# Second cross-attention of a perceiver stack: three PSUM places for scores, a split last chunk and another order around the maximum

## The reference, cut to what matters

```python
scale = 1.0 / np.sqrt(ATT_DIM).astype(np.float32)
Q = jnp.einsum('bld,de->ble', input_1, Wq) + bq
K = jnp.einsum('bld,de->ble', input_2, Wk) + bk
V = jnp.einsum('bld,de->ble', input_2, Wv) + bv
scores = jnp.einsum('bqd,bkd->bqk', Q, K) * scale
scores = jnp.clip(scores, -100.0, 100.0)
weights = jax.nn.softmax(scores, axis=-1)
return jnp.einsum('bqk,bkd->bqd', weights, V)
```

## Time and profile before

| | us |
|---|---|
| median of 3 runs | 1199.65 |
| lowest and highest | 1196.90, 1203.51 |
| the profiled execution, device time | 1200.66 |
| its span in the profile | 1198.9 |
| TensorE / VectorE / ScalarE / GpSimd busy, share of the span | 95% / 76% / 75% / 49% |
| mean granted TensorE clock | 0.993 |

### The profile page before, as it was taken

The page is one execution under the profiler, slowest core; times in us unless marked ns, Lnnn a source line. Parts: engine busy times, 40 slices in busy tenths (PEclk is TensorE's granted clock), DMA queues, the critical chain, the costliest instruction groups (busy, mean ns, idle before and its releaser), DMA issues. The chain is left out here.

```text
span 1198.9 us, 32157 instructions
## 1 busy us (share of the span) xinstructions
PE 1144.7 (95%) x12519; PEld 795.4 (66%) x12519; DVE 909.6 (76%) x1739; ACT 902.8 (75%) x1557; POOL 586.9 (49%) x548
## 2 busy tenths in 40 slices
PE   4899999999999999999999999999988999889898
PEld 2466666666666666666666666666666648744698
DVE  7677878888888888888878787877774689689632
ACT  4599988888988889888888888888881459495010
POOL 6165656665666665656556666656561250133000
PEclk8999999999999999999999999999999899999999
DMA  6365544545353535353535353534335884050284
GB/s 217 84 180 165 157 122 99 146 95 152 92 152 90 154 95 155 92 149 91 155 94 154 92 151 90 154 94 124 91 98 175 309 311 146 10 177 1 95 288 173
DMA packets 141428, 163.93 MB, mean 137 GB/s; under 512 B 18352, under 2 KB 127184, under 8 KB 141280
## 3 DMA queue, kind: packets, MB, share of 16 engines
q1 hardware_dynamic: 140736, 159.82, 46.4%
q10 hardware_dynamic: 544, 2.10, 0.5%
HBM read 72.25 MB, written 12.99 MB: 71 GB/s over the span
## 5 line engine op out<-in xcount | busy, mean ns | idle before, releaser
L468 POOL TENSOR_TENSOR pT_lo<-p_exp,pT_hi 128x896 f16<-128x896 f32 x223 | 421.3, 1889 | 319.4 <-ACT pT_hi L568 319.4
L549 ACT ACTIVATE p_exp<-ps,ln_k,esc 128x896 f32<-128x896 f32 x224 | 246.3, 1100 | 54.0 <-PE ps L910 46.1
L682 DVE TENSOR_REDUCE tile_max<-ps 128x128 f16<-128x896 f32 x224 | 244.4, 1091 | 49.5 <-PE ps L886 47.1
L568 ACT ACTIVATE pT_hi<-p_exp 128x896 f16<-128x896 f32 x224 | 211.9, 946 | 1.0
L677 DVE TENSOR_TENSOR v_lo<-ps,v_hi 128x512 f16<-128x512 f32 x196 | 135.5, 691 | 72.9 <-ACT v_hi L541 70.6
L928 PE MATMUL ps<-v_lo,pT_hi 128*128 128x64 f16 x1568 | 164.4, 193 | 0.0
L927 PE MATMUL ps<-v_hi,pT_hi 128*128 128x65 f16 x1568 | 164.3, 193 | 0.1
L873 PE MATMUL ps<-c_hi,wk_hi 128*128 128x448 f16 x448 | 159.1, 355 | 5.4 <-DVE c_lo L664 4.7
L929 PE MATMUL ps<-v_hi,pT_lo 128*128 128x65 f16 x1568 | 163.8, 193 | 0.0
L873 PE MATMUL ps<-c_lo,wk_hi 128*128 128x448 f16 x448 | 158.4, 354 | 0.0
L873 PE MATMUL ps<-c_hi,wk_lo 128*128 128x448 f16 x448 | 158.4, 354 | 0.0
(11 more groups left out here) (401 smaller groups left out, 2080.9 us busy)
## 6 DMA issues: line engine op xcount, KB each, us to landing
k_st<-k_top SPq DMA_DIRECT2D x444, 112.0 KB, 2.3
k_st<-k_rest SPq DMA_DIRECT2D x444, 56.0 KB, 2.0
c_raw<-in_ctxT SPq DMA_DIRECT2D x14, 896.0 KB, 5.9
xa_cn<-in_ctx SPq DMA_DIRECT2D x14, 896.0 KB, 6.6
me_w<-in_me_w SPq DMA_DIRECT2D x8, 1536.0 KB, 6.3
ctx_parts<-c_hi SPq DMA_DIRECT2D x14, 448.0 KB, 2.8
ctx_parts<-c_lo SPq DMA_DIRECT2D x14, 448.0 KB, 3.0
me_w<-in_me_w SPq DMA_DIRECT2D x8, 768.0 KB, 5.8
```

The source lines that it names most:

```text
L468: nc.gpsimd.tensor_tensor(pT_lo[:, n % 2, :, :].rearrange("p t s -> p (t s)"), p_exp[:, n % 2, :], pT_hi[:, n % 2, :, :].rearrange("p t s ...
L549: nc.scalar.activation(p_exp[:, n % 2, :], s_scores[n % 2], ACT.Exp, bias=ln_k[:, 0:1], scale=esc[:, n // H0 % 2:n // H0 % 2 + 1]).then_in ...
L568: nc.scalar.activation(pT_hi[:, n % 2, :, :].rearrange("p t s -> p (t s)"), p_exp[:, n % 2, :], ACT.Copy).then_inc(pT_hi_ready, 1)
L682: nc.vector.tensor_reduce(tile_max[:, n % 2, :], s_scores[n % 2].rearrange("p (t s) -> p s t", s=S), AX.X, ALU.max).then_inc(tile_max_done, 1)
```

## The change

PSUM has a third place for scores, banks 0 and 1, and TensorE waits for the chunk three back. The last two chunks are clipped after the maximum, not the last alone. The last chunk's matmuls are done one bank after the other, each counted in `scores_done`, and its maximum is taken by halves into `ends`; the maximum of the first 13 chunks is formed before. The turned tiles go to banks 0 to 3 in place of 2 to 5. VectorE makes the low parts of the first four tiles before those of the last three, and TensorE begins to weigh with the four tiles while the three are waited for at the fifth.

```diff
-        total = t("total", [P, NCH])
+        total, ends = t("total", [P, NCH]), t("ends", [P, 2])
...
-        sc_ps = [ps[:, 2:4, 0:HCH], ps[:, 4:6, 0:HCH]]
-        t_ps = [[ps[:, 2, :], ps[:, 3, :]], [ps[:, 4, :], ps[:, 5, :]]]
+        sc_ps = [ps[:, b:b + 2, 0:HCH] for b in (2, 4, 0)]
+        t_ps = [[ps[:, 0, :], ps[:, 1, :]], [ps[:, 2, :], ps[:, 3, :]]]
+        CLIPS_FIRST = NCH - 2
+        measured_all = 2 * CLIPS_FIRST + 1
...
                 def exponent(c):
...
-                    if c == NCH - 1:
-                        act.wait_ge(E["clipped"], 2 * NCH)
+                    if c >= CLIPS_FIRST:
+                        act.wait_ge(E["clipped"], measured_all + c - CLIPS_FIRST + 1)
...
                 def measure(c):
...
-                    nc.vector.tensor_reduce(chunk_max[:, c:c + 1], sc_ps[c % 2], AX.XY, ALU.max).then_inc(E["clipped"], 1)
+                    nc.vector.tensor_reduce(chunk_max[:, c:c + 1], sc_ps[c % 3], AX.XY, ALU.max).then_inc(E["clipped"], 1)
...
                 def clip(c):
...
-                    nc.vector.tensor_scalar(sc[:, c * CH:(c + 1) * CH].rearrange("p (b k) -> p b k", b=2), sc_ps[c % 2],
+                    nc.vector.tensor_scalar(sc[:, c * CH:(c + 1) * CH].rearrange("p (b k) -> p b k", b=2), sc_ps[c % 3],
...
-                for c in range(NCH - 1):
+                for c in range(CLIPS_FIRST):
...
-                measure(NCH - 1)
-                v.wait_ge(E["clipped"], 2 * NCH - 1)
+                measure(NCH - 2)
+                v.wait_ge(E["clipped"], measured_all)
+                link(nc.vector.tensor_tensor(chunk_max[:, 0:NCH - 1], chunk_max[:, 0:NCH - 1], f[:, 0:NCH - 1], ALU.mult))
+                link(nc.vector.tensor_reduce(top[:, :], chunk_max[:, 0:NCH - 1], AX.X, ALU.max))
+                link(nc.vector.tensor_scalar(top[:, :], top[:, :], lim[:, 0:1], None, ALU.max))
+                for b in range(2):
+                    v.wait_ge(E["scores_done"], NCH + b)
+                    link(nc.vector.tensor_reduce(ends[:, b:b + 1], sc_ps[(NCH - 1) % 3][:, b, :], AX.X, ALU.max))
                 marks["top"] = link.count + 1
-                link(nc.vector.tensor_tensor(chunk_max[:, :], chunk_max[:, :], f[:, :], ALU.mult))
-                link(nc.vector.tensor_reduce(top[:, :], chunk_max[:, :], AX.X, ALU.max))
-                link(nc.vector.tensor_scalar(top[:, :], top[:, :], lim[:, 0:1], lim[:, 1:2], ALU.max, ALU.min))
+                link(nc.vector.tensor_scalar(ends[:, 0:1], ends[:, 0:1], ends[:, 1:2], f[:, NCH - 1:NCH], ALU.max, ALU.mult))
+                link(nc.vector.tensor_scalar(top[:, :], ends[:, 0:1], top[:, 0:1], lim[:, 1:2], ALU.max, ALU.min))
                 nc.vector.tensor_scalar(neg_top[:, :], top[:, :], -1.0, LN_K, ALU.mult, ALU.add).then_inc(E["top_ready"], 1)
+                clip(NCH - 2)
                 clip(NCH - 1)
...
                     link(nc.vector.tensor_copy(pT_hi[:, c % 2, T0:TILES, :], turned[1]))
-                    nc.vector.tensor_tensor(pT_lo[:, c % 2, T0:TILES, :], turned[1], pT_hi[:, c % 2, T0:TILES, :], ALU.subtract).then_inc(E["pT_ready"], 1)
                     v.wait_ge(E["pT_hi_ready"], c + 1)
                     nc.vector.tensor_tensor(pT_lo[:, c % 2, 0:T0, :], turned[0], pT_hi[:, c % 2, 0:T0, :], ALU.subtract).then_inc(E["pT_ready"], 1)
+                    nc.vector.tensor_tensor(pT_lo[:, c % 2, T0:TILES, :], turned[1], pT_hi[:, c % 2, T0:TILES, :], ALU.subtract).then_inc(E["pT_ready"], 1)
...
-                    at_least(pe, E["clipped"], 2 * (c - 1))
-                    for k in range(DC):
-                        if c == 0:
-                            pe.wait_ge(E["q2_ready"], k + 1)
-                        for q2, low in ((q2_hi, 0), (q2_hi, 1), (q2_lo, 0)):
-                            for b in range(2):
-                                mm = nc.tensor.matmul(sc_ps[c % 2][:, b, :], q2[:, k, :], ct[:, low, k, b * HCH:(b + 1) * HCH],
-                                                      start=(k == 0 and low == 0 and q2 is q2_hi), stop=(k == DC - 1 and q2 is q2_lo))
-                    mm.then_inc(E["scores_done"], 1)
-                pe.wait_ge(E["clipped"], 2 * NCH - 2)
-                spin(nc, spare, ident, 4)
-                keep_warm(nc, pe, spare, ident, vlink.sem, marks["top"], marks["top"] + 2)
+                    at_least(pe, E["clipped"], 2 * (c - 2))
+                    for bs in ((0, 1),) if c < NCH - 1 else ((0,), (1,)):
+                        for k in range(DC):
+                            if c == 0:
+                                pe.wait_ge(E["q2_ready"], k + 1)
+                            for q2, low in ((q2_hi, 0), (q2_hi, 1), (q2_lo, 0)):
+                                for b in bs:
+                                    mm = nc.tensor.matmul(sc_ps[c % 3][:, b, :], q2[:, k, :], ct[:, low, k, b * HCH:(b + 1) * HCH],
+                                                          start=(k == 0 and low == 0 and q2 is q2_hi), stop=(k == DC - 1 and q2 is q2_lo))
+                        mm.then_inc(E["scores_done"], 1)
+                pe.wait_ge(E["clipped"], measured_all)
+                spin(nc, spare, ident, 3)
+                keep_warm(nc, pe, spare, ident, vlink.sem, marks["top"], marks["top"] + 1, 2)
...
                 def turn_p(c):
...
-                        pe.wait_ge(E["clipped"], 2 * NCH)
+                        pe.wait_ge(E["clipped"], measured_all + 1)
...
                 def weigh(c):
...
-                    pe.wait_ge(E["pT_ready"], 2 * c + 2)
+                    pe.wait_ge(E["pT_ready"], 2 * c + 1)
                     for tile in range(TILES):
+                        if tile == T0:
+                            pe.wait_ge(E["pT_ready"], 2 * c + 2)
...
```

## The result

| | before | after |
|---|---|---|
| median of 20 runs, us | 1199.15 | 1196.94 |
| lowest and highest | 1196.14, 1203.57 | 1194.37, 1200.41 |
| the profiled execution, device time | 1200.66 | 1194.58 |
| its span | 1198.9 | 1192.9 |

The ratio of the changed kernel to the kernel before is 0.9972, 95% interval 0.9961 to 0.9983: 3.4 us less, between 2.0 and 4.7. The two medians in the table are 2.2 us apart. The forecast was 3.1. Times of this size tell that the change gains something; how much it gains is read inside the block.

The account below looks back on a forecast made before the run. Waits between VectorE and TensorE over two PSUM places bound the scores pass, VectorE the weighing; 2.14 + 0.47 + 0.48 = 3.1 us off 1199.65 gives a median of 1196.6, range 1193.3 to 1200.2.

Parts of the forecast that it names:

- Third place: Scores pass: TensorE no longer waits for a clip to free its PSUM place; last scores end 1.70 us earlier.
- Around the maximum: From chunk 12's measure to neg_top: half maxima at 0.62 each; neg_top starts 2.14 us earlier, 2.0 to 2.3 with bounds.
- Two clips behind: After neg_top: the second clip fills VectorE's 1.22 us idle before the first cast; costs nothing, at worst 0.1.
- Order of the split: Weighing pass: low part of four tiles comes first; first weighing 0.47 us earlier, 0.48 more at the end.
- Sum: Whole block: 2.14 + 0.47 + 0.48 = 3.1 us less; the median becomes 1196.6 us.
- no difference: Whole kernel: the measurement cannot tell the change from none, bound about 0.5%; chance 0.87.
- What follows: Behind the block: ended by a barrier, its loads hang on its own steps, so it moves as a whole.
- A: Scores pass: the third place frees nothing, as loads or issue hold TensorE; gain 1.5 us, 1198.1; chance 0.10.
- B: Weighing pass: TensorE's wait at the fifth tile costs 3.9 us over 13 chunks; gain 0.4, 1199.2; chance 0.10.
- C: Scores pass or stretch before the first weighing: TensorE's clock falls; up to 31.8 us, 1228.3; chance 0.03.
- the loads: Scores pass: chunk 13's column load lands with 2.3 us of slack before TensorE wants it; costed at nothing.

Follow-up runs that it names:

- the kernel before with warming matmuls: Six identity matmuls added to TensorE's idle time in the feed-forward block ahead, on the kernel before; median 1200.13 us, ratio to before 0.9984.
- late columns: Changed kernel with the column loads of chunks 11 to 13 issued two chunks later each; 1198.21 us in one run, block 80.50 us.

## Why the prediction was right

**Third place.** Predicted 1.70 earlier, with TensorE as the bound; measured 31.17 to 29.47, and 1.69 of the block when done alone. The releaser that I took from the clip's end plus 0.11, against the view's "issue", was right: with two places the pauses came back.

**Around the maximum.** Predicted neg_top 2.14 earlier, measured 2.09. The halves were taken at 0.62 each from the 384 and 512 rows; the two take 1.28 with the gap between them, which is the same. The clamp with one limit took 0.24 with its gap, not 0.20, and the two operations before it 0.45, not 0.44. That is the missing 0.05.

**Two clips behind.** Predicted at nothing; measured nothing, by the cast at 2.49 behind neg_top with one clip and with two. It fits by 0.1 us.

**Order of the split.** Predicted 0.47 at the front and 0.48 at the end, nothing between. Measured 0.44 at the first weighing; from there to the last addition 46.01 became 45.56, 0.45, and to the last weighing 40.70 became 40.25, where 40.2 was forecast. Alone 0.86, within the change 0.89.

**Sum.** 3.09 predicted, 2.98 in the block, 3.4 (2.0 to 4.7) by the ratio. The sums of parts agree: 1.69 + 0.86 for place and order alone leave 0.43 for the early maximum, the halves and the clip together, which measured 0.40. That leaves 0.03 for the turned tiles' other banks, which have no run of their own. The forecast median, 1196.6, came within 0.4 of the 1196.94 measured; that is luck in part, since it was built on a median of three runs and the 20 runs lie 7.4 us apart for the kernel before and 6.0 for the changed one. The 3.09 against 2.98 in the block is the test of the mechanism. By the 0.5% that the prediction took as its bound, 0.28% is no difference, the case to which it gave 0.87.

**What follows** moved as a whole: 162.64 after, 162.56 before.

**Rivals.** A fell (two places make the pauses return). What A would have left, a gain of 1.5, measured 1.26 with two places, as neg_top then came 0.38 earlier and not 0.56. B fell: the fifth tile starts without a gap in every chunk, and the order alone shortens the block. C fell: the clock is 1.00 from the first measure to the last scores, with TensorE busy 29.50 of 29.50 us, and from there to the first weighing. The Trainium skill's rule on going round PSUM banks (TensorE: Matmul & The Clock Gate, "A second HAM failure mode: psum-queue depth-cycling") does not show in the traces of this case: the clock stayed at 1.00 with two places and 13 pauses, and with three places the pauses are gone.

**What was mis-sized** is a term costed at nothing. I gave the loads 2.3 us of slack on the row of 8.0 us from issue to landing. In the changed kernel the load took 10.3, and the slack was 0.9. It hid the loads all the same. By these numbers a scores pass another microsecond faster would meet them, which is an estimate.

## What to carry to other kernels

Where two engines hand a pair of buffers back and forth and the pass is slower than either engine's own need, look at the buffers: here a third place gained the number of chunks times the difference to the slower engine, 13 x (2.40 - 2.27) = 1.70 us, and this could be read off one timeline. Splitting an instruction so that it can start earlier pays when its engine is free at that moment: with the clip still in front, the halves and the early small operations made the maximum 0.60 us later; with the clip moved away they made it 0.40 earlier. When the effect is a few microseconds in a scatter of eight, measure it between two points within the block.

## What the runs showed that I had not expected

The block's length repeats within 0.03 us while the program's time varies by 5 and more. A good part of that scatter goes with stretches where TensorE's clock is at 1.2 GHz: of the 20 runs of the changed kernel the three with a mean granted clock of 0.991 or 0.992 took 1199.0 to 1200.4 us, and the eight at 0.995 or 0.996 took 1194.4 to 1195.7 (the one at 0.997 does not fit, at 1197.1). In the feed-forward block such a stretch starts after one with much idle time, and it comes and goes between runs of one kernel; there it costs 0 to 4.2 us (24.9 to 29.1), and 2.65 of the 6.0 us between the two profiled spans are this.

The last load of context columns lands 26.2 us after the first measure whether it is issued at 15.9 (the change, 10.3 to landing), at 16.7 (the kernel before with warming matmuls, 9.5) or at 20.4 (late columns, 5.8). In the profile of before that the prediction used it landed at 24.7 with the issue at 16.7, and so it did with two places; in the other eleven profiles it landed at 26.0 to 26.5. Why these two were earlier is open; a slack read from one row was good to 1.5 us.
